# An 8-core sandwich layer: the down-projection weights loaded in three pieces inside the first gate/up loop instead of at the start, and the input tiles counted in four groups

## The reference

```python
def attn(x, bind_key, unbind_key, gate, decay):
    bound = circ_conv(x, bind_key)
    d = sigmoid(decay)
    decay_matrix = where(t >= s, d ** (t - s), 0)
    hologram = einsum('ts,bsd->btd', decay_matrix, bound)
    return x + gate * circ_corr(hologram, unbind_key)

def ffn(x, w_gate, w_up, w_down):          # 3072 hidden, int32 weights times 1/127
    gate = x @ wg.T ; up = x @ wu.T
    return (silu(gate) * up) @ wd.T

x = x + layernorm(attn(layernorm(x)))
x = x + layernorm(ffn(layernorm(x)))
```

## Time and profile before

| | |
|---|---|
| median of 2 runs | 862.88 us (862.68 to 863.08) |
| profiled execution, its own time | 864.42 us |
| its span, first to last instruction, slowest core (core 1) | 862.9 us |
| spans of the eight cores | 856.8 to 862.9 us |
| PE busy | 670.2 us (78%) |
| DVE busy, ACT busy | 237.1 us (27%), 227.9 us (26%) |
| DMA, mean over the span | 62 GB/s |

### The profile page before, as it was taken

One profiled execution on the slowest core, in us unless ns is written; L12 is line 12 of the kernel. 1 busy time (PEld: TensorE's weight loads), 2 busy tenths in 40 slices (PEclk: granted clock), 3 DMA queues, 4 the chain that ended last, 5 costly groups with the idle time before them and its releaser, 6 DMA issues.

```text
span 862.9 us, 8416 instructions; the slowest of 8 cores (856.8 to 862.9 us)
## 1 busy us (share of the span) xinstructions
PE 670.2 (78%) x3024; PEld 297.2 (34%) x3024; DVE 237.1 (27%) x579; ACT 227.9 (26%) x325; POOL 29.1 (3%) x58
## 2 busy tenths in 40 slices
PE   0093047899960069979999999879899999999994
PEld 0041012234420034434444444344344444444441
DVE  0000840005555621441211113233212121112223
ACT  2031065424443241131112122333211111212222
POOL 1000000000000000000000000000000000000000
PEclk9997566669995569989999999969999999999998
DMA  9999400000000204424444401101544444410111
GB/s 191 179 172 205 148 0 0 1 1 2 0 1 0 49 1 73 74 50 74 73 74 76 78 20 49 49 25 50 90 81 74 74 74 74 76 22 25 50 49 73
DMA packets 12281, 53.40 MB, mean 62 GB/s; under 512 B 1376, under 2 KB 1376, under 8 KB 11728
## 3 DMA queue, kind: packets, MB, share of 16 engines
q0 software_dynamic: 7632, 36.08, 25.2%
q1 hardware_dynamic: 4608, 16.78, 5.8%
HBM read 80.12 MB, written 8.39 MB: 103 GB/s over the span
## 4 chain that ended last, share of the span: by engine, by line
PE 64%; DVE 8%; SPq 7%; ACT 7%; issue 7%; DMA 5%; DVEq 0%; ACTq 0%; POOLq 0%
PE pg L630 19%; PE pu L638 18%; PE pu L707 10%; PE pf L707 10%; SPq L64 7%; PE pb L359 4%; DMA x<-xin 4%; ACT t1a L434 2%; DVE sqd L413 2%; ACT xw L316 2%; PE pt L573 2%; ACT t1a L406 1%; PE pb L354 1%; DVE sta L538 1%; DVE x2t L577 1%
## 5 line engine op out<-in xcount | busy, mean ns | idle before, releaser
L630 PE MATMUL pg<-x2t,wgu 128*128 128x512 bf16 x768 | 179.2, 388 | 12.1 <-DVE xw L657 5.8
L638 PE MATMUL pu<-x2t,wgu 128*128 128x512 bf16 x768 | 173.6, 379 | 0.0
L651 ACT ACTIVATE sil<-pg,z 128x512 bf16<-128x512 f32 x96 | 65.4, 687 | 244.6 <-PE pg L630 244.6
L630 PEld LDWEIGHTS pg<-x2t,wgu 128*128 128x128 bf16 x768 | 75.8, 100 | 109.0 <-issue 24.3
L638 PEld LDWEIGHTS pu<-x2t,wgu 128*128 128x128 bf16 x768 | 75.1, 98 | 90.6
L657 DVE SCALAR_TENSOR_TENSOR xw<-sil,pu 128x512 bf16<-128x512 bf16 x64 | 43.6, 687 | 171.6 <-PE pu L638 169.5
L359 PE MATMUL pb<-l0b,xw 128*128 128x512 bf16 (+3 forms) x128 | 35.8, 438 | 48.2 <-ACT xw L316 48.2
L476 PE MATMUL pr<-hc,zt 128*128 128x512 bf16 x256 | 62.9, 390 | 7.5 <-ACT t1a L406 6.6
L235 PE MATMUL cp<-cubb,cbtb 128*128 128x512 bf16 x128 | 29.9, 399 | 41.4 <-DMA cubb<-cuT 41.4
L573 PE MATMUL pt<-idb_s,x2s 128*128 128x128 bf16 x128 | 15.3, 294 | 59.1 <-ACT x2s L563 45.9
L707 PE MATMUL pf<-wdtb,xw 128*128 128x512 bf16 x256 | 57.9, 379 | 2.1 <-DVE hc L657 2.1
(11 more groups left out here) (91 smaller groups left out, 463.5 us busy)
## 6 DMA issues: line engine op xcount, KB each, us to landing
wgu<-wgu POOLq DMA_DIRECT2D x48, 512.0 KB, 5.3
x<-xin SPq DMA_DIRECT2D x16, 512.0 KB, 62.3
out<-x SPq DMA_DIRECT2D x16, 512.0 KB, 2.6
wdtb<-wdt POOLq DMA_DIRECT2D x1, 6144.0 KB, 78.8
cbtb<-cbt POOLq DMA_DIRECT2D x1, 2048.0 KB, 23.3
cubb<-cuT POOLq DMA_DIRECT2D x1, 2048.0 KB, 37.4
cstf_s<-cstf POOLq DMA_DIRECT2D x1, 257.0 KB, 8.8
cstb_s<-cstb POOLq DMA_DIRECT2D x1, 128.0 KB, 8.9
```

Of the source, the lines that this page charges most:

```text
L630: pe_g[eta][c] = op("tensor", lambda e, sl=sl, c=c, d=d: e.matmul(PG[sl][:, 512 * c:512 * c + 512], WGU[sl][:, 128 * d:128 * d + 128], X2T ...
L638: pe_u[eta][c] = op("tensor", lambda e, sl=sl, c=c, d=d: e.matmul(PU[sl][:, 512 * c:512 * c + 512], WGU[sl][:, 1024 + 128 * d:1024 + 128 * ...
L651: sc_sil[eta][c] = op("scalar", lambda e, sl=sl, c=c: e.activation(SIL[sl][:, 512 * c:512 * c + 512], PG[sl][:, 512 * c:512 * c + 512], AF ...
```

## The change

The load of `WDTB` leaves POOL's list at the head and comes back as three loads of a third each (8192 of 24576 columns), issued in half 0 right after the loads of the gate/up blocks 7, 13 and 19. The down-projection waits for all three. The loads of X keep their order and their queue, but are counted on four semaphores of four tiles each instead of two of eight, and DVE waits for one of them ahead of tiles 0, 4, 8 and 12. Nothing else is changed; no engine computes more or less than before.

```diff
     for t in range(TN):
-        dma("sync", X[t][:], xin[:, 1024 * t:1024 * t + 1024], "LDX" if t < 8 else "LDX2")
-    ld_allx = 8 * 16
-    ld_allx2 = C["LDX2"]
+        dma("sync", X[t][:], xin[:, 1024 * t:1024 * t + 1024], f"LDX{t // 4 + 1}".replace("LDX1", "LDX"))
+    ldx_tot = [4 * 16] * 4
 
     dma("gpsimd", CBTB[:], cbt[:, :], "WCC")
     wt_ccin = dma("gpsimd", CUBB[:], cuT[:, :], "WCC")
-    wt_wd = dma("gpsimd", WDTB[:], wdt[:, :], "WWD")
+    wt_wd = 3 * 16
...
         t = g
-        if t == 0:
-            w("vector", "LDX", ld_allx)
-        if t == 8:
-            w("vector", "LDX2", ld_allx2)
+        if t % 4 == 0:
+            w("vector", f"LDX{t // 4 + 1}".replace("LDX1", "LDX"), 64)
...
             if hf == 0 and eta == 6:
                 dv_ln2_done = emit_ln2(1, dv_ln2_done)
+            if hf == 0 and eta in (7, 13, 19):
+                g = (7, 13, 19).index(eta)
+                dma("gpsimd", WDTB[:, 8192 * g:8192 * g + 8192],
+                    wdt[:, 8192 * g:8192 * g + 8192], "WWD")
```

More of the change, by code:

```diff
@@ L39, in build_nc @@
     plan = {k: [] for k in ("sync", "gpsimd", "vector", "scalar", "tensor")}
-    C = {"LDX": 0, "LDX2": 0, "LDC": 0, "WCC": 0, "WWD": 0, "WG0": 0, "WG1": 0,
-         "PE": 0, "DV": 0, "SC": 0, "GP": 0, "ST": 0}
+    C = {"LDX": 0, "LDX2": 0, "LDX3": 0, "LDX4": 0, "LDC": 0, "WCC": 0, "WWD": 0,
+         "WG0": 0, "WG1": 0, "PE": 0, "DV": 0, "SC": 0, "GP": 0, "ST": 0}
     S = {}
```

## The result

| | before | with the change |
|---|---|---|
| median | 863.18 us (8 runs) | 854.56 us (9 runs, 852.37 to 856.44) |
| ratio to before | | 0.9895, interval 0.9881 to 0.9909 |
| profiled execution, its own time | 864.42 us | 852.37 us |
| spans of the cores in it | 856.8 to 862.9 us | 840.3 to 850.8 us |

The change makes the kernel 1.05% faster, 8.6 us by the medians. The forecast was 844.8 us, 18.1 us less than before, and the range ended at 852: the direction was right, the size a little under half of what was forecast.

The account below looks back on a forecast made before the run. The head was taken as bound by bytes on the DMA engines, the gate/up loop by TensorE. A 40.4 us gain less a 22.3 us loop cost gave 862.88 - 18.1 = 844.8 us, range 838 to 852.

Parts of the forecast that it names:

- The head: Stretch up to the scan: without WDTB X lands earlier, the root waits for HC's last copy instead, 40.4 us gained.
- The loop: Gate/up loop of half 0: blocks queued behind the thirds wait and the clock drops, costing 22.3 us.
- Block 8: Gate/up block behind the first third: lands at 381.4 against 379.24 wanted, a wait of 2.2 us.
- Blocks 14 and 20: Gate/up blocks behind the second and third thirds: wait 7.6 and 8.1 us for them in queue 0.
- Clock: Gate matmuls after the two new gaps of near 8 us: slower clock costs 2.2 us each, 4.4 us.
- The sum: Whole kernel: 40.4 us gained in the head less 22.3 lost in the loop, 862.88 - 18.1 = 844.8 us.
- The Trainium skill's rule: DMA queues: descriptors within one ring go in order, so splitting into thirds doesn't protect gate/up blocks on POOL's queue.
- The estimate from the formula of that page (Anatomy of one DMA): Loop: a third takes about 9.6 us rather than 12.6, loop some 9 us cheaper, result an estimated 836 us.
- The loop hides more: Loop: engines mix a third with the following block, about 5 us cost for all three, 827.5 us; 7%.
- X becomes late: Head: X at 205 GB/s beside the circulants lands at 69.3, gain only 35.4 us, 849.8 us; 8%.
- X is paced by its own queue: Head: X's last landing stays at 98.15, only the smaller last group helps, 6.4 us; 878.8 us, slower; 3%.
- The thirds take longer in the loop: Loop: each third takes 14.6 us instead of 12.6, giving 850.8 us; 12%.

Follow-up runs that it names:

- the count of pieces: Changed kernel with WDTB loaded in the loop in 24, 6, 3 or 1 pieces: 824.35, 834.21, 849.90 and 850.11 us.
- eight small DMAs: Changed kernel with each third of WDTB still read from HBM, but in eight DMAs of 128 x 1024: 856.50 us, ratio 0.9935.
- two groups: Changed kernel with X counted in two groups of eight tiles again, the thirds kept: 851.37 us, ratio 0.9868.
- Reading from SBUF: Changed kernel with the thirds read from tiles of X in SBUF instead of HBM, eight DMAs a third: 844.06 us, ratio 0.9803.
- The repeated run: Changed kernel once more, unaltered: 849.90 us, ratio 0.9859 to the kernel before.
- WDTB whole: Changed kernel with WDTB loaded in one piece behind gate/up block 7 instead of in thirds: 850.11 us, single run.

## Why the prediction was wrong, step by step

**The head** was right as a mechanism and close in size. Forecast: X complete at 61.4, DVE's input at 69.2, the root at 72.1 behind HC's last copy, the scan at 79.2, 40.4 us gained. Measured: X by 58, the root at 71.12, the scan at 78.23, 40.7 us sooner than before on core 3. CUBB came 0.9 us sooner, inside the bound. What the working lacked is that the new bound is a stretch of dense matmuls whose clock is not always 1.00: by the lengths above, 1 to 3 us of the gain are gone where it falls to 0.81.

**The loop** is the step that failed: the mechanism was right, the size not. The thirds do stand ahead of blocks 8, 14 and 20 in queue 0, as the count of pieces shows. Block 8 before the change, on core 3 and on core 5:

```profile
377.25 5.67 PE L630 MATMUL pg<-x2t,wgu 128*128 128x512 bf16 x16 [5.57 <-DVE xw L657]
...
375.44 6.22 PE L630 MATMUL pg<-x2t,wgu 128*128 128x512 bf16 x16 [5.77 <-DVE xw L657]
```

The sum, term by term on core 3 against its own rows of before:

- Block 8: 9.68 - 5.57 = 4.1 us, forecast 2.2. Blocks 14 and 20: 8.87 and 9.41, forecast 7.6 and 8.1. Together 22.4 instead of 17.9.
- Blocks 7, 13 and 19: 1.01 + 0.91 + 0.69 = 2.6 us, forecast none. I took the block that is issued ahead of a third to land undisturbed after 5.4 us; block 7 took 6.9.
- Clock: 0.9 + 1.33 + 2.03 = 4.3 us, forecast 4.4.

That is 29.3 of the 29.5 us. On core 5 the same terms are 3.0 + 8.25 + 7.57 of waiting and 4.4 of clock, 23.2 of 23.3. The 12.6 us for a third hold there: its landing at 17.4 from its issue. On core 3 block 8 landed 325.56 + 16.8 = 342.4, block 7 at 318.65 + 6.9 = 325.5, so third and block took 16.9 us and not 15.8. The wrong step is therefore the one by which rows of an undisturbed loop and of the head gave one price for all eight cores: a third at 12.6 us and 17.9 us of waiting, and nothing at all for the blocks ahead of the thirds, where the slower core of a pair measured 13.7 us a third, 22.4 us of waiting and 2.6 us for those blocks. The trace of before already held a sign: core 1 has a wait of 0.40 us for wgu before block 4, and core 5 has none.

Which core of a pair pays more was the same in every kernel: the one whose loop began later, in 24 of 24 pairs of the six profiles with one, three or six pieces, eight small DMAs or two groups (where the first matmul's record is missing, its start is taken one matmul earlier). By its own count it begins 0.1 to 3.1 us later and issues its block 7 1.1 to 4.6 us later. These counts start at each core's own first instruction. Where the clock of a pair fell to 0.81, the fall stands 0.20 to 0.21 us apart in the times of the two and lasts equally long; if it is one event for both, their counts differ by no more than that, and at block 7 the order of the two is firm. The pairing is not made by the thirds alone: in the other six profiles the later core has the longer loop too, in 21 of 24 pairs, by 0.2 to 3.4 us. Reading from SBUF took most of the split away, so the neighbours disturb each other in what they read from HBM. Why the later one loses so much more than the earlier one, and what sets the size, stays open.

**The sum.** On the slowest cores of the profiled execution it is 40.7 - 29.5 = 11.2 us against 18.1; the execution's own time moved by 12.05. The other 8 executions of the first nine lie 1 to 4 us higher, and have no profile; clock and neighbours are candidates, neither is shown for them. The repeated run gave 12.5 us by its medians.

**The rivals.** "The loop hides more" was excluded by the count of pieces. "X becomes late" and "X is paced by its own queue" were wrong: X ran at 305 to 336 GB/s from 40 us on (windows of 4 us on core 3). "The thirds take longer in the loop" came nearest: I gave 850.8 and 12%, and thought of the transfer alone. The range had its upper end near there, and the result lies 2.6 us outside. It lacked the blocks ahead of the thirds, 2.6 us on core 3, and the clock of the circulants, which stood at 1.00 in the profiled execution; that these two make up the difference in the others is not shown.

**The Trainium skill's rule** on the order within one ring (DMA: Bandwidth & Descriptors, Queues, rings and completion order) held: what the prediction drew from it, that the split into thirds doesn't protect the blocks behind them, is what the waits of 7.6 to 9.7 us show. The estimate from the formula of that page (Anatomy of one DMA), 836 us, was further off than the sum from the rows: a third took 12.6 and 13.7 us here, and not 9.6.

## What to carry to other kernels

Moving a load out of a crowded head pays in full only if the place it moves to has a DMA queue that is empty again when the next urgent load is issued: look for a stretch without transfers first (here about 60 to 240 us, worth some 37 us, where the change won 9 to 12), and if it must share the queue of a double-buffered loop, cut it so that a piece passes within the slack of one block. Price a shared resource on the worst core, not on one: neighbours that are nearly alike before can disturb each other at exactly the moments that the change adds. And before crediting a gain to the large half of a change, cost the small half alone; four groups instead of two, two waits of DVE more in all, were worth some 8 us by themselves, and 0 to 2 beside the other half.

## What the runs showed of the hardware

TensorE's granted clock fell to 0.81, between its two usual levels, for 4.6 to 15.2 us in the middle of continuous 128 x 512 matmuls, in ten of twelve profiles: for the same time on both cores of a pair in all of these, on all four pairs in three of them, and on one to two pairs in the others (the table above). With SBUF as the source it fell once more, for 4.1 us at 564 us, on cores 6 and 7. In none of the twelve did it fall so in the gate/up loop of half 0, with matmuls on all cores. The Trainium skill (TensorE: Matmul & The Clock Gate, Seeing it yourself) tells of a limiter that takes a whole die to 13/16 when three of its cores run dense matmuls, for as long as the load lasts. The level agrees with that. That cores 6 and 7 fell once without 4 and 5, that some executions with the same load show nothing, and that the clock came back with the matmuls going on, does not.

Gaps of 7 to 10 us in the loop cost between 1.3 and 3.0 us of slower clock in the 16 matmuls behind them (4.94 to 6.57 us instead of 3.61 in the six on cores 3 and 5, whose mean cost is 2.2). The price does not grow with the gap: in all twelve profiles together, gaps of 5.5 to 6.5 us cost 1.3 to 2.9, those of 7 to 11.3 us 1.3 to 3.0, and the eight of 32.8 to 34.3 us, with WDTB whole, 1.3 to 2.8.
